# Routed experts run on sorted row tiles instead of on every row

## The reference, cut to what matters

```
def _route(x, gate_weight):
    scores = sigmoid(x @ gate_weight.T)                # (T, 16)
    top2, _ = top_k(scores.reshape(T, 4, 4), 2)
    _, gidx = top_k(top2.sum(-1), 2)                   # 2 of 4 groups
    masked = where(mask of those groups, scores, 0.0)
    topk_idx = top_k(masked, 4)[1]
    topk_w = take_along_axis(scores, topk_idx, axis=1)
    topk_w = topk_w / (topk_w.sum(-1, keepdims=True) + 1e-20) * 2.5
    combine = zeros((T, 16)).at[arange(T)[:, None], topk_idx].add(topk_w)
...
up = einsum('th,ehi->eti', x, expert_up)               # (16, T, 128)
down = einsum('eti,eih->eth', silu(up), expert_down)   # (16, T, 256)
moe_out = einsum('te,eth->th', combine, down)
shared = silu(x @ shared_up) @ shared_down             # 512 wide
x = x + gb * (moe_out + shared)
```

## Time and profile before

| what | us |
|---|---|
| median of 3 runs (2582.83 to 2591.03) | 2590.68 |
| span of the profiled execution, first to last instruction | 2587.5 |
| PE busy | 2394.4 |
| DVE busy | 1655.0 |
| ACT busy | 1109.5 |
| POOL busy | 616.3 |

### The profile page before, as it was taken

How to read it: one execution, slowest core, us unless ns; L and a number is a source line. 1 busy time by engine, 2 the same in 40 slices (tenths; PEclk the granted TensorE clock), 3 DMA queues, 4 the chain that set the end, 5 groups by cost and what they waited for, 6 DMA issues and landing times.

```text
span 2587.5 us, 41994 instructions
## 1 busy us (share of the span) xinstructions
PE 2394.4 (93%) x14594; PEld 1659.7 (64%) x14594; DVE 1655.0 (64%) x4354; ACT 1109.5 (43%) x2350; POOL 616.3 (24%) x417
## 2 busy tenths in 40 slices
PE   6899997667897999979999999999999999999998
PEld 4466665555676888845666666666666666666665
DVE  4487886449922566525767676667667676766675
ACT  2477876346663222224334424433443344244331
POOL 1145554031101111211312231222123132312210
PEclk9999998787667999989999999999999999999999
DMA  5447556978767767421202210220122022101000
GB/s 166 162 149 219 174 166 192 270 212 203 212 155 223 217 204 225 156 74 49 58 1 58 58 50 9 58 58 13 45 59 58 1 58 58 43 15 58 9 9 8
DMA packets 376312, 272.14 MB, mean 105 GB/s; under 512 B 199714, under 2 KB 333794, under 8 KB 373906
## 3 DMA queue, kind: packets, MB, share of 16 engines
q1 hardware_dynamic: 371474, 243.85, 33.6%
q0 software_dynamic: 4640, 25.73, 2.9%
HBM read 168.60 MB, written 100.93 MB: 104 GB/s over the span
## 4 chain that ended last, share of the span: by engine, by line
PE 43%; DVE 9%; issue 3%; POOL 2%; ACT 0%; DMA 0%; DVEq 0%; SPq 0%; POOLq 0%; ACTq 0%
PE mx_dn L2002 16%; PE mx_up L1988 15%; PE mx_m L1938 4%; DVE mx_acc L2316 4%; PE mx_m L1965 2%; POOL mx_rms L1894 2%; PE mx_m L1942 1%; PE mx_m L1979 1%; DVE hl L2224 1%; DVE mx_st L2214 1%; DVE hl L2199 1%; DVE hl L2188 1%; DVE mx_rms L2193 1%; PE mx_m L1973 1%; PE mx_m L1947 1%
## 5 line engine op out<-in xcount | busy, mean ns | idle before, releaser
L2316 DVE SCALAR_TENSOR_TENSOR mx_acc<-mx_dn,mx_comb,mx_acc 128x256 f32<-128x256 f32 x1024 | 424.3, 478 | 356.6 <-PE mx_dn L2002 352.7
L2002 PE MATMUL mx_dn<-mx_edn,mx_hs 128*128 128x256 f32 x2048 | 487.7, 381 | 0.0
L1988 PE MATMUL mx_up<-mx_h2T,mx_eup 128*128 128x512 f32 x1024 | 484.3, 595 | 0.0
L2002 PEld LDWEIGHTS mx_dn<-mx_edn,mx_hs 128*128 128x128 f32 x2048 | 384.4, 190 | 145.6 <-issue 91.0
L2090 ACT ACTIVATE mx_hs<-mx_up 128x512 f32<-128x512 f32 x320 | 190.8, 596 | 625.8 <-PE mx_up L1988 625.1
L1988 PEld LDWEIGHTS mx_up<-mx_h2T,mx_eup 128*128 128x128 f32 x1024 | 190.9, 190 | 156.1 <-issue 145.2
L675 DVE SCALAR_TENSOR_TENSOR cv_acc<-cv_pre,conv_w,cv_acc 128x512 f32<-128x512 f32 x288 | 215.7, 750 | 78.2 <-ACT cv_acc L597 71.3
L539 PE MATMUL cv_pj<-cv_hT,wqkv 128*128 128x512 f32 x384 | 181.8, 604 | 12.7 <-ACT cv_acc L597 7.7
L713 POOL TENSOR_TENSOR rn<-cv_ss,half_pow 128x8 f32 x64 | 127.5, 1992 | 13.2 <-POOL cv_ss L709 13.2
L1880 POOL TENSOR_TENSOR mx_st<-mx_tmp,root_pow 128x24 f32<-128x24 f32 x30 | 124.6, 4168 | 20.1 <-DVE mx_tmp L2142 20.1
L1938 PE MATMUL mx_m<-mx_hT,wr 128*128 128x512 f32 x256 | 122.2, 601 | 3.3 <-DMA mx_x<-_attn_hidden_states_dram 2.5
(11 more groups left out here) (292 smaller groups left out, 3998.7 us busy)
## 6 DMA issues: line engine op xcount, KB each, us to landing
kqT_d<-cv_kqc SPq DMA_DIRECT2D x16, 1024.0 KB, 8.5
vf_d<-cv_vf SPq DMA_DIRECT2D x16, 1024.0 KB, 5.4
fl_toep<-taps_d SPq DMA_DIRECT2D x32, 392.0 KB, 7.3
ds_kqT<-kqT_d SPq DMA_DIRECT2D x10, 1024.0 KB, 5.9
fl_v<-vf_d SPq DMA_DIRECT2D x8, 1216.0 KB
ci_kT<-kqT_d POOLq DMA_DIRECT2D x19, 512.0 KB, 5.7
fl_d<-fl_out POOLq DMA_DIRECT2D x8, 1029.0 KB, 7.2
xin<-_attn_hidden_states_dram SPq DMA_DIRECT2D x16, 512.0 KB, 4.3
```

Of the source, the lines that this page charges most:

```text
L1988: ins = pe.matmul(up_ps[x % 2][:], lhs, h2T[i][:, k, :], start=(k == 0), stop=(k == KD - 1))
L2002: ins = pe.matmul(dn_ps[(i + n) % 2][:, j, :], hs[x % 4][:, j * P:(j + 1) * P], rhs, start=(x == 0 and j % 2 == 0) or x >= NS, stop=(x >= ...
L2316: ins = dve.scalar_tensor_tensor(out=acc[i][:, j, :], in0=dn_ps[(i + n) % 2][:, j, :], scalar=comb[i][:, j, e:e + 1], in1=acc[i][:, j, :], ...
```

## The change

Routed experts no longer run on all rows. The rows of two units (`GU` = 2, a group) are sorted by expert through DRAM, run in 48 tiles of 128 rows (`TILES`), and gathered back. Of each unit, in order:

- The mixing, the gate and the shared expert stay, as steps s of the unit; the residual x2 plus gb times the shared expert goes to DRAM (`base_d`). The normalized rows, before scale and shift, are kept in `xn`, a ring of three units.
- `route` leaves ranks; `slots` picks the four chosen scores in rank order, their weights `wts`, and with two matmuls (against a triangle and against ones) each row's place among the rows of its expert. For each group `places` turns the counts into whole tiles per expert, the slot of each row and rank (`idx`) and the expert of each of the 48 tiles (`ei`).
- POOL scatters the rows with 32 indirect DMAs a group into `xg_d`. The 48 tiles then run one per beat: SP reads the tile's expert into a register and loads its rows, its up weights and its down weights; PE transposes the rows, DVE (even tiles) or ACT (odd ones) evicts them with scale and shift; up, Silu, down, copy to `og`, stored to `yg_d`.
- POOL gathers each row's four results from `yg_d` with indirect DMAs, 16 a unit, and DVE adds them to the loaded base by weight; SP stores the unit.

Everything is issued by beats, in one list per engine with no loop: unit u is at step s = beat - 24u, its steps -16 to 68; tile n is turned at beat 96 + n, its up is in the next beat, its down in the one after. There are 546 beats, 96 before the first tile and 66 after the last. `dense` and POOL's finish are gone. Expert weights are no longer loaded in `delta_scan`; at the start of the new stage, beside the first units, SP and POOL read expert_down, multiply it by each batch's gate and write it to `dn_d`, and clear the row buffers. Three earlier stages declare some of their semaphores elsewhere so that they can be cleared and used again; POOL clears those of `chunk_inverses` as `delta_scan` begins.

```diff
+GU = 2
+TILES = GU * UT * TOPK // P + E
...
-                if 9 <= t < 9 + KD:
-                    k = t - 9
-                    sp.dma_start(m.eup[:, k], w.expert_up[:, k * P:(k + 1) * P, :].rearrange("e p i -> p e i"))\
-                        .then_inc(m.w_in, 16)
-                if t == TB - 1:
-                    sp.wait_ge(std_done, 2)
-                    sp.dma_start(m.edn[:], w.expert_down.rearrange("e i h -> i e h")).then_inc(m.w_in, 16)
...
+            for s in m.inverse_sems:
+                pool.sem_clear(s)
...
+    T = TILES
+    NGR = NU // GU
+    PER = T // GU
+    TB0 = (GU - 1) * PER + 72
+    NTILE = NGR * T
+    RX, RO, RG, RN, ZT = 6, 6, 2, GU + 1, 8
+    LX = 3
+    END = TB0 + NTILE + 6 + GU * PER + 12
...
+        def sums_from(v):
+            return TB0 + T * (v // GU + 1) + 6 + PER * (v % GU)
...
+            def load_tile(n):
+                g, t, i = n // T, n % T, n % RX
+                b = g * GU // UB
+                if n == 0:
+                    for y in two:
+                        sp.wait_ge(ed_out[y], 16 * E // 2)
+                if t == 0:
+                    sp.wait_ge(tab_done, g + 1)
+                    sp.wait_ge(scat_out[g % 2], 256 * GU * (g // 2 + 1))
+                if n >= RX:
+                    sp.wait_ge(d_done, n - RX + 1)
+                e = sp.value_load(ei[g % 2][0:1, t:t + 1], min_val=0, max_val=E - 1)
+                sp.dma_start(xg[i][:], m.xg_d[g % 2][t * P:(t + 1) * P, :]).then_inc(tile_in[i], 16)
+                sp.dma_start(ew[i][:, 0:KD * EI].rearrange("p (k i) -> p k i", k=KD),
+                             up_v[bass.ds(e, 1)].squeeze(0)).then_inc(tile_in[i], 16)
+                sp.dma_start(ew[i][:, KD * EI:], m.dn_d[b, bass.ds(e, 1)].squeeze(0)).then_inc(tile_in[i], 16)
+
+            def put_tile(n):
+                g, t = n // T, n % T
+                sp.wait_ge(og_done, n + 1)
...
+                sp.dma_start(m.yg_d[g % 2][t * P:(t + 1) * P, :], og[n % RO][:]).then_inc(og_out[n % RO], 16)
...
+            for beat in range(END):
+                n = tile_at(beat, -LX)
+                if n is not None:
+                    load_tile(n)
+                n = tile_at(beat, 3)
+                if n is not None:
+                    put_tile(n)
+                for u, s in live(beat):
+                    unit(u, s)
...
+            def scatter(g, q):
...
+                pool.indirect_dma_start(m.xg_d[g % 2], bass.IndirectOffsetOnAxis(idx[:, c:c + 1], 0), xn[u % RN][:, j, :], None)\
+                    .then_inc(scat_out[g % 2], 16)
...
+            def gather(v, q):
+                c, r = v * J + q // TOPK, q % TOPK
+                if q == 0 and v % GU == 0:
+                    last = (v // GU + 1) * T
+                    for i in range(RO):
+                        pool.wait_ge(og_out[i], 16 * len(range(i, last, RO)))
+                if r == 0 and c >= RG:
+                    pool.wait_ge(comb_step, TOPK * (c - RG + 1))
+                y = c * TOPK + r
+                pool.indirect_dma_start(gb_in[c % RG][:, r, :], None, m.yg_d[v // GU % 2], bass.IndirectOffsetOnAxis(idx[:, y:y + 1], 0))\
+                    .then_inc(g_in[c % RG], 16)
...
-            def up(u, i, x):
...
+            def turn(n):
+                i = n % RX
+                pe.wait_ge(tile_in[i], 48 * (n // RX + 1))
+                if n >= 1:
+                    pe.wait_ge(xt_done, n)
                 for k in range(KD):
...
+                    ins = pe.transpose(tp_ps[:, k * P:(k + 1) * P], xg[i][:, k * P:(k + 1) * P], m.ident[:])
+                ins.then_inc(t_done, 1)
+
+            def up(n):
+                pe.wait_ge(xt_done, n + 1)
+                if n >= 1:
+                    pe.wait_ge(ht_done, n)
+                for k in range(KD):
+                    ins = pe.matmul(up_ps[:, 0:P], ew[n % RX][:, k * EI:(k + 1) * EI], xgT[n % 2][:, k, :],
+                                    start=(k == 0), stop=(k == KD - 1))
+                ins.then_inc(u_done, 1)
+
+            def down(n):
+                pe.wait_ge(ht_done, n + 1)
+                if n >= 1:
+                    pe.wait_ge(og_done, n)
+                pe.matmul(dn_ps[:, 0:D], ht[n % 2][:], ew[n % RX][:, KD * EI:], start=True, stop=True).then_inc(d_done, 1)
...
+            for beat in range(END):
+                n = tile_at(beat, 0)
+                if n is not None:
+                    turn(n)
+                units = live(beat)
+                for u, s in units[:1]:
+                    unit(u, s)
+                n = tile_at(beat, 1)
+                if n is not None:
+                    up(n)
+                for u, s in units[1:]:
+                    unit(u, s)
+                n = tile_at(beat, 2)
+                if n is not None:
+                    down(n)
...
+            def combine(v, q):
...
+                dve.scalar_tensor_tensor(out=o[:, j, :], in0=gb_in[c % RG][:, r, :], scalar=wts[:, c, r:r + 1],
+                                         in1=o[:, j, :], op0=ALU.mult, op1=ALU.add).then_inc(comb_step, 1)
```

More of the change, by code:

```diff
@@ L1736, in mix_and_experts @@
[L1736 to L1742, removed]
+        wsel = sb("mx_wsel", [P, J, TOPK])
+        wts = sb("mx_wts", [P, NT, TOPK])
@@ new lines, in mix_and_experts @@
+        runs = sb("mx_runs", [P, GU * J + 1, E])
+        slot = [sb(f"mx_slot{i}", [P, J, E]) for i in range(GU)]
+        idxf = sb("mx_idxf", [P, J, TOPK])
+        idx = sb("mx_idx", [P, NT * TOPK], i32)
+        cnt = sb("mx_cnt", [P, E])
+        cmp = sb("mx_cmp", [P, E, E])
+        ntl = sb("mx_ntl", [P, E])
+        before = sb("mx_before", [P, E])
+        upto = sb("mx_upto", [P, E])
+        own = sb("mx_own", [P, T, E])
+        tile_e = sb("mx_tile_e", [P, T])
+        ei = [sb(f"mx_ei{i}", [P, T], i32) for i in two]
@@ new lines, in _ @@
+            for beat in range(END):
+                for u, s in live(beat):
+                    unit(u, s)
+                e, late = divmod(beat - 10, 4)
+                if late == 0 and 0 <= e < E:
+                    scale_down(e)
+                for v in range(NU):
+                    x = beat - sums_from(v)
+                    for q in range(J * TOPK):
+                        if x == q * PER // (J * TOPK):
+                            gather(v, q)
+            for y in two:
+                pool.wait_ge(scat_out[y], 128 * NU)
@@ new lines, in keep @@
+            def keep(n):
+                act.wait_ge(d_done, n + 1)
+                if n >= RO:
+                    act.wait_ge(og_out[n % RO], 16 * (n // RO))
+                act.activation(og[n % RO][:], dn_ps[:, 0:D], ACT.Copy).then_inc(og_done, 1)
+            for beat in range(END):
+                n = tile_at(beat, 0)
+                if n is not None and n % 2:
+                    turn(n)
+                units = live(beat)
+                for u, s in units[:1]:
+                    unit(u, s)
+                n = tile_at(beat, 1)
+                if n is not None:
+                    silu(n)
+                for u, s in units[1:]:
+                    unit(u, s)
+                n = tile_at(beat, 2)
+                if n is not None:
+                    keep(n)
@@ L2346, in _ @@
             dve.tensor_reduce(pick[:], m.ident[:].rearrange("p (f a) -> p a f", a=GR)[:, 0:3 * H, :], AX_X, ALU.add)\
                 .then_inc(pick_done, 1)
[L2348 to L2349 removed]
+            dve.wait_ge(const_done, 2)
+            for beat in range(END):
+                n = tile_at(beat, 0)
+                if n is not None and n % 2 == 0:
+                    turn(n)
+                units = live(beat)
+                for u, s in units[:1]:
+                    unit(u, s)
+                for u, s in units[1:]:
+                    unit(u, s)
+                for v in range(NU):
+                    x = beat - sums_from(v) - PER // J - 2
+                    for q in range(J * TOPK):
+                        if x == q * PER // (J * TOPK):
+                            combine(v, q)
```

943 lines of the change are left out of this document (562 added, 381 removed).

## The result

The changed kernel takes 2776.4 us (median of four runs, 2766.2 to 2778.6) against 2587.9 (four runs, 2582.8 to 2591.0): a ratio of 1.072, 95% interval 1.069 to 1.075. The profiled span is 2764.4 us against 2587.5, 177 more; the forecast was 126 more (2717 us, with 2640 to 2800 as its own range). The 2764.4 belong to the shortest of the four runs; the median is 10 us above it.

A forecast was written before the change was run, and what follows sets the result against it. PE bounds the old stage (1477 us); afterwards five coupled engines would wait on each other. Front 225 + 14 rounds x 84 + lone tiles 144 + end 58 = 1603, +126 us: 2717 us, own range 2640 to 2800, full range 2470 to 2930.

The forecast's parts named there:

- its own signs: Round some 84 us, PE well below 85%, SP unpaused, 3.2 us a tile, first transposes after 225, indirect DMAs near 1.2.
- the 14: Rounds of 24 beats, tiles beside units' work, between front and lone tiles: 84 us each, from 70 to 121.
- the front: From the new stage's start to the first tile, beats 0 to 95: 225 us (190 to 250).
- a lone tile: After the rounds, 48 tiles alone at SP's pace: 3.0 us each, 144 in all; the sign named some 3.2.
- the second rival: POOL late in scatter beats: indirect DMA at 1.9 us, rounds 96.5 each, +301 us, 2892; chance 0.13.
- The break-even: Round length at which new and old stage take equal time: 75 us, with 427 us outside the 14 rounds.
- 50 + 3 x 58: Sum for the beats before the first tile, with two units sharing engines from beat 24: 225 us.
- I cost these at nothing: New waits on scatters, stored tiles, gathers and POOL's powers, with the engines behind them: priced at zero.
- SP (-17 with the end): SP's issues, register load and waits: 3.2 us a tile, sum 85 a unit; lone tiles 144, end 58.
- PE as the bound: Rival: PE still bounds the rounds, 72 us each, 102 us less, 2488; chance 0.34.
- Clogged rings: Rival: SP or the DMA rings clog, 105 us a round, 3.6 a lone tile, +449 us, 3040; chance 0.11.

The follow-up runs named there:

- POOL's roots: Changed kernel with POOL's two square roots of a unit turned into plain products (results change): 2703.7 us, ratio 1.043.
- by phase: Kernel of "pairs, roots on ScalarE", with VectorE evicting up to beat 10 of each 24 and ScalarE after it: 2557.8 us, ratio 0.990.
- pairs, roots on ScalarE: Changed kernel with tiles loaded, evicted and stored two at a time, loads five beats ahead, and both roots on ScalarE instead of POOL: 2584.5 us, ratio 0.999.
- the longer lead: Changed kernel with tile loads asked for five beats ahead instead of three, eight input buffers instead of six: 2720.3 us, ratio 1.051.

## Why the prediction was right, and what it mis-sized

**The mechanism was right, the terms less so.** PE stopped being the bound, its units' work and the tiles' short steps on five engines wait for each other beat by beat, and rounds lose what the experts gave. Two of its own signs came: rounds near 84 (85.8 over the 14), PE well under 85% (841 of 1072 us, 78%). Others did not: the front took 265 us and not 225, a lone tile 2.71 and not 3.2, SP's queue paused for 189 us of the rounds (139 of them for a free buffer), and POOL ran almost without gaps in the first half of a scatter round, which had been named as a sign of the second rival. The time lies 24 us below the upper end of the forecast's own range.

The experiments show separate losses: 3.7 us a round from SP's lead, 4.3 from POOL's roots, 10.7 when pairs and roots are mended together, 12.3 with the evictions placed by phase. The break-even held: it was a round of 75 us with 427 us outside the 14 rounds. With 75.7 and 407 (pairs, roots on ScalarE) the time is that of the kernel before, with 74.1 and 403 (by phase) it is below.

**Mis-sized: the front (+40, the largest term).** The step "50 + 3 x 58" failed in its 58: unit 0 came to its projection after 47 us, but the next three took 66.0, 73.5 and 69.3. The scaling of 16 expert weights with the gate, on POOL and with 32 transfers, was left out of the sum; taking it away gave 18 us. Without the roots on POOL the front was 7 us shorter, with pairs and the roots on ScalarE 11. If these add, some 11 to 15 of the 40 us are left. PE's longest waits in the front, 1114 to 1379, say where to look:

```profile
PE mx_b L2146 <- DVE mx_on L2434: 79.5, 4, 24.4
PE mx_a L2111 <- POOL mx_st L2023: 23.6, 3, 12.6
```

The first is the chain of a unit's own mixing, on which PE and VectorE take turns; what sets its length was not measured.

**Mis-sized: "I cost these at nothing".** The prediction named POOL's powers and who waits for them, and priced them at nothing, because it looked at single late instructions and at POOL's sum for a whole round (76 us of 84), and not at the first half of a scatter round. PE waits 52 us for the roots in the rounds and 24 in the front. That is the second rival's mechanism in part; its price was not: an indirect DMA takes 1.07 us on the mean and 0.30 to the next, 1.37 in all against the 1.2 taken and the rival's 1.9.

```profile
L2081 POOL DMA_INDIRECT mx_g<-yg_d,mx_idx x256 | 271.4, 1060 | 412.9 <-DVE mx_ob L2641 327.7
...
L2062 POOL DMA_INDIRECT xg_d<-mx_xn,mx_idx x256 | 277.6, 1084 | 125.8 <-issue 74.0
```

**Mis-sized the other way: SP (-17 with the end).** SP's issues in the lone tiles of the kernel after:

```profile
2640.03 0.33 SPq L1936 DMA_DIRECT2D mx_xg<-xg_d  x1
2640.55 0.40 SPq L1937 DMA_DIRECT2D mx_ew<-in_L_ffn_expert_up_dram  x1
2641.13 0.34 SPq L1939 DMA_DIRECT2D mx_ew<-dn_d  x1
2641.51 0.43 SPq L1947 DMA_DIRECT2D yg_d<-mx_og  x1
2642.55 0.33 SPq L1936 DMA_DIRECT2D mx_xg<-xg_d  x1
```

A tile's cycle is 2.52 us where nothing waits (2.71 on the mean of the lone tiles), not 3.2. From the first issue to the end of the last it is 1.91, and 0.61 holds the waits and the register load, which the prediction took at 0.7. The issues were priced too high: 1.9 us for four, where 2.5 was taken from rows of a stage with other transfers. The register load has a row of its own, all 384 of them (shortest, median and longest in ns):

```profile
L1935 SPq TENSOR_LOAD <-mx_ei x384: 262/268/923, 1367.0 to 2702.1; - x192
```

The Trainium skill (DMA: Bandwidth & Descriptors, Latency and other measured facts) gives such a load a floor of about 600 ns; here the median is 268 ns, so the floor does not hold in this kernel.

So SP needs 24 x 2.52 + 8.7 = 69 us a round and not 85, and was no bound of a round by itself; the longer lead mended its lateness in light beats. That the rounds still came out within 2 us of 84 is luck in part: SP's sum was 16 us too high, and POOL's lateness, put at nothing, took 4.3 us a round, and the two light rounds at the end, which the sum put at 84 as well, bring the mean from 89.1 down to 85.8.

**The rivals.** PE as the bound: no, PE is idle 231 us in the rounds. Clogged rings: no, the issues of tiles stay at 0.33 to 0.43 us on the median, at some 235 GB/s, and the longer lead took away 63 of the 77 us for which PE waited for loads.

## What to carry to other kernels

When work leaves the bounding engine, add up the others beat by beat and not only by the round: POOL was busy 68 of 98 us and still late, since its first half was full. Count every preparatory operation that a change adds ahead of its loop; here 16 uncounted products with their transfers cost 18 us. A short operation on which PE waits belongs to the engine that has no long run of its own work in that phase, and that may be another engine in another phase.

## What the hardware showed

**An indirect DMA waits for a two-input VectorE operation.** Of the 512 in the kernel after, 279 have no two-input operation of VectorE beside them and take 0.97 us on the median, 1.16 at most. Here are POOL's timeline of the kernel after, and VectorE's at the same time, 1024-wide operations with two inputs from SBUF:

```profile
1703.38 2.36 POOL L2062 DMA_INDIRECT xg_d<-mx_xn,mx_idx  x1 [0.30 <-issue]
1706.04 1.85 POOL L2062 DMA_INDIRECT xg_d<-mx_xn,mx_idx  x1 [0.30 <-issue]
```

```profile
1703.67 1.22 DVE L2419 TENSOR_TENSOR hl<-hl,kv 128x1024 f32<-128x1024 f32 x1
...
1705.84 1.22 DVE L2423 TENSOR_TENSOR hl<-hl,kv 128x1024 f32<-128x1024 f32 x1
```

They end 0.85 and 0.83 us after the operation beside them. The Trainium skill (SBUF — State Buffer, SBUF: two separate sides) says that a VectorE operation with two inputs from SBUF blocks a GpSimd operation that reads SBUF until it ends; the trace agrees if the indirect DMA counts as one for its indices, which lie in SBUF. All 49 that take over 1.3 us end 0.82 to 0.93 us after such an operation of 1024 columns, while the eight that began under `mx_acc<-mx_b,gbB`, as wide but with one input from PSUM, took 0.94 to 1.01. It is rare enough to leave the mean at 1.07 us. It is read from the trace; no run took it away.

**The clock was higher where PE waited less.** With fewer waits the granted clock of the rounds, a mean near the upper of its two levels (1.2 and 2.4 GHz), rose from 0.88 (after) to 0.91 and 0.92 (roots, phase). How much of each gain this is was not separated. The end of the delta scan came between 1109 and 1123 us in the seven profiles with the same code up to there, so a difference of some 10 us between two profiles ahead of the stage means nothing.
